# A two-layer graph network on one core: the softmax chain of a batch moved four visits later in two of three edge passes

## The reference, cut to what matters

```
m = segment_max(logits, dst); e = exp(logits - m[dst]); s = segment_sum(e, dst)
out = segment_sum(h[src] * (e / s[dst]), dst)
...
alpha = sum(xs_j * a_s) + sum(xd_i * a_d); alpha = where(alpha >= 0, alpha, 0.2 * alpha)   # layer 1
out = segment_sum(xs_j * (a * edge_weight), dst)
```

## Time and profile before

| | us |
|---|---|
| median of 3 runs | 4023.07 (4012.54 to 4028.57) |
| the profiled execution | 4020.69 |
| its span | 4018.8 |
| busy: PE / DVE / POOL / ACT | 2935.1 / 3088.3 / 2729.9 / 1446.3 |
| pass 1: first gather issued, last addition | 145.7 to 1206.2 |
| pass 3: first gather issued, last addition | 2562.9 to 3625.3 |
| mean of one L284: pass 1, 2, 3 | 1.002, 0.948, 1.006 |
| granted TensorE clock, mean | 0.85 of full |

### The profile page before, as it was taken

How to read it: one execution, slowest core, us unless ns; L and a number is a source line. 1 busy time by engine, 2 the same in 40 slices (tenths; PEclk the granted TensorE clock), 3 DMA queues, 4 the chain that set the end, 5 groups by cost and what they waited for, 6 DMA issues and landing times. The chain is left out here.

```text
span 4018.8 us, 70607 instructions
## 1 busy us (share of the span) xinstructions
PE 2935.1 (73%) x14389; PEld 2089.2 (52%) x14389; DVE 3088.3 (77%) x9652; ACT 1446.3 (36%) x4590; POOL 2729.9 (68%) x2963
## 2 busy tenths in 40 slices
PE   5456666677777677788888888466676677777998
PEld 4334444444455455555555556334444444447998
DVE  6567777788897666677777769678888899997886
ACT  2322233233326456666666666211111111112332
POOL 3577777777750277777777735577777777755886
PEclk8677777778878889999999989677778878888999
DMA  4555555555534444444444437555555555533221
GB/s 131 164 158 163 162 159 161 173 165 169 173 106 120 138 135 136 136 140 137 141 141 141 142 87 221 166 143 147 145 144 147 149 149 149 151 102 92 72 72 50
DMA packets 271620, 560.27 MB, mean 139 GB/s; under 512 B 62118, under 2 KB 164558, under 8 KB 271278
## 3 DMA queue, kind: packets, MB, share of 16 engines
q0 software_dynamic: 115872, 326.30, 29.0%
q10 hardware_dynamic: 82742, 167.20, 13.3%
q1 hardware_dynamic: 72664, 63.00, 5.4%
HBM read 478.39 MB, written 77.89 MB: 138 GB/s over the span
## 5 line engine op out<-in xcount | busy, mean ns | idle before, releaser
L475 PE MATMUL psum<-big,onehots_or_distances 128*128 128x264 f32 (+2 forms) x5280 | 1851.1, 476 | 101.9 <-DVE big L656 55.4
L475 PEld LDWEIGHTS psum<-big,onehots_or_distances 128*128 128x128 f32 x5280 | 1008.2, 223 | 281.2 <-DVE big L656 82.4
L284 POOL DMA_INDIRECT big<-table_attn,src_by_edge x782 | 741.5, 948 | 437.2 <-issue 238.0
L284 POOL DMA_INDIRECT big<-table_typed,src_by_edge x782 | 786.8, 1006 | 249.8 <-issue 237.9
L284 POOL DMA_INDIRECT big<-table_gat,src_by_edge x782 | 783.3, 1002 | 252.6 <-issue 231.8
L341 ACT ACTIVATE dot_products<-big 128x8 f32 (+1 forms) x880 | 156.5, 213 | 1562.1 <-SPq L274 1483.1
L679 DVE TENSOR_TENSOR acc<-acc,psum 128x264 f32 (+2 forms) x1320 | 558.5, 423 | 105.9 <-issue 58.6
L656 DVE TENSOR_TENSOR big<-big,psum 128x512 f32<-128x512 f32 x880 | 594.1, 675 | 14.1 <-issue 4.9
L438 PE MATMUL psum<-big,onehot_t 128*128 x2640 | 462.8, 285 | 155.1 <-SPq L274 91.7
L521 DVE SCALAR_TENSOR_TENSOR dot_products<-psum,big 128x258 f32<-128x258 f32 x880 | 367.6, 421 | 191.0 <-PE psum L438 186.4
L438 PEld LDWEIGHTS psum<-big,onehot_t 128*128 128x128 bf16 x2640 | 260.9, 101 | 362.0 <-issue 247.0
(11 more groups left out here) (284 smaller groups left out, 4243.8 us busy)
## 6 DMA issues: line engine op xcount, KB each, us to landing
onehot_t<-onehots ACTq DMA_DIRECT2D x73, 512.0 KB, 3.8
big<-visit_positions ACTq DMA_DIRECT2D x55, 512.0 KB
onehots<-big ACTq DMA_DIRECT2D x37, 512.0 KB, 5.9
big<-onehots ACTq DMA_DIRECT2D x37, 512.0 KB, 3.6
big<-in_x_dram SPq DMA_DIRECT2D x98, 128.0 KB, 2.7
big<-table_gat,src_by_edge POOLq DMA_INDIRECT x782
big<-table_attn,src_by_edge POOLq DMA_INDIRECT x782
big<-table_typed,src_by_edge POOLq DMA_INDIRECT x782
```

What stands on the lines that cost most here:

```text
L284: pool.indirect_dma_start(X[:, t % RING, :], None, ph.table, bass.IndirectOffsetOnAxis(ap=m.src[:, t:t + 1], axis=0)).then_inc(S[f"rows{t ...
L475: last = nc.tensor.matmul(sum_ps(w), onehot_at(v), rows, start=(v % 2 == 0), stop=(v % 2 == 1))
```

## The change

CHAIN_AHEAD becomes 0 for passes 1 and 3 (pass 2 does not use it). The chain's places then are the visits: it begins four visits later, `shift` goes from place 15 to 11 and so stays at visit 11, the parts from `scan_ahead` to `join_last` move from places 5..10 to 3..8 (from visits 1..6 to 3..8), and `turn_max` from place 11 to 9 (from visit 7 to 9). The expansions, the turn of the logits and the tail copies move four visits later with the batch. No instruction is added or removed, and no wait.

```diff
-        self.max_at = 13 if self.dot else 11
+        self.max_at = 13 if self.dot else 9
...
-CHAIN_AHEAD = 4
+CHAIN_AHEAD = 0
...
-                (5, 1, scan_ahead), (5, 1, scan_back), (6, 1, ends), (6, 1, turn_ends), (7, 1, run_scans), (7, 1, from_others),
-                (8, 1, join), (8, 1, carry), (9, 1, turn_joined), (9, 1, join_first), (10, 1, join_last),
-                (15, 1, shift)])
+                (3, 1, scan_ahead), (3, 1, scan_back), (4, 1, ends), (4, 1, turn_ends), (5, 1, run_scans), (5, 1, from_others),
+                (6, 1, join), (6, 1, carry), (7, 1, turn_joined), (7, 1, join_first), (8, 1, join_last),
+                (11, 1, shift)])
```

## The result

The changed kernel takes **3995.16 us** (median of 4 runs, 3986.40 to 3998.30) against 4024.80 for the kernel before in the same comparison (4 runs): ratio **0.9928 [0.9901, 0.9955]**, 29.6 us less. The forecast was 3963, 60 us less. The sign was right, the size half of what was forecast.

The account below looks back on a forecast made before the run. POOL's gather issue, lengthened by L644, was taken to bound passes 1 and 3. Terms -31 - 22 - 4.6 - 5 = -63 us, taken as -60 from 4023.1, gave 3963 us; range 3940 to 3998.

Parts of the forecast that it names:

- What bounds the kernel: Passes 1 and 3: POOL's issue of gathers sets them, 18.6 us a batch; VectorE has 2 to 3 us to spare.
- Delay = 0.55 less the distance, by L644: A gather starting within 0.55 us behind an L644 is lengthened by 0.55 us less its distance.
- The first rival: Passes 1 and 3: delays travel with the chain or come of something other than L644; -10 us, 4013; chance 0.13.
- otherwise none: Gathers that don't start within 0.55 us behind an L644 aren't lengthened: delay 0.
- Pass 1, -31 us: Pass 1: the moved L644 leave 0.2 us of gather delay a batch, 11 us for 41.7.
- Pass 3, -22 us: Pass 3: the first L644 still catches a gather, 0.42 us a batch, 23 us of delay for 45.3.
- Room in the ring, -4.6: Pass 1: POOL's twenty waits for ring room lose their 4.6 us at most, as VectorE has used up four visits more.
- The ends, -5: Ends of passes 1 and 3: plain work of four visits is already done, 2.5 us each, -5 us.
- What gets tighter, 0: Growth to shift, leaky to scan, and ScalarE's weighing have less time; cost 0, up to 2 us a batch covered.
- A check from the other side: Passes 1 and 3: L644 meeting gathers at random gives 26 us of delay a pass; random placing would give -45 us.
- the worst case of the known rule: Passes 1 and 3: a batch can lose 0.5 + 0.15 us, 35 us a pass; 17 us still gained, 3996.

Follow-up runs that it names:

- e1: Changed kernel, with pass 1's L644 reading iota from PSUM instead of SBUF: 3961.31 us, ratio 0.9847.
- e2: Kernel before the change, with pass 1's L644 reading iota from PSUM: 4000.57 us, ratio 0.9942.
- e8: Changed kernel, with L644 reading iota from PSUM in passes 1 and 3, and three sums in flight instead of four in pass 3: 3951.00 us, 0.9830.
- e5: Changed kernel, with ScalarE's two 512 KB transfers of a batch in pass 1 issued eight visits later: 4018.75 us, ratio 0.9998.
- e6: e5 with ScalarE's two long conversions of pass 1 also eight visits later: 4019.09 us, ratio 1.0004.
- e14: e9 with LAG = 8 instead of 9 in all passes: 3963.90 us, ratio 0.9857.
- e13: e8 with LAG = 8 instead of 9: 3919.66 us, ratio 0.9746.
- e17: Kernel before the change, with e13's edits (iota in PSUM in both passes, LAG = 8): 3943.64 us, ratio 0.9798.
- e11: Changed kernel, with ScalarE's weighing at v % 16 = 9 instead of 13 in passes 1 and 3: 3994.84 us, ratio 0.9919.
- e12: Changed kernel, with pass 1's chain two visits later than in the kernel before instead of four (CHAIN_AHEAD = 2): 4050.63 us, ratio 1.0052.
- e9: Changed kernel, with each of pass 1's four L644 waiting for VectorE's own instruction ahead to be complete: 3985.83 us, ratio 0.9894.
- e15: e12 with each L644 of pass 1 waiting for VectorE's own instruction ahead to be complete: 3960.15 us, ratio 0.9848.
- e4: Changed kernel, with growth (L621) as one scalar_tensor_tensor instead of tensor_scalar: 4013.30 us, ratio 0.9975.

## Why the prediction was right or wrong, point by point

- **What bounds the kernel: right.** Passes 1 and 3 go by POOL's issue of gathers; what shortened gathers shortened them.
- **Delay = 0.55 less the distance, by L644: right, but taken too narrowly.** e1, e2 and e8 show it: with one SBUF operand the delays are gone. The first rival, which the Trainium skill's inference ("SBUF — State Buffer", section "Who interferes with whom") spoke for, is contradicted by them: by it the operand could have changed nothing, and it decides over 51 us of busy time in pass 1 (792.9 to 742.2). But the rule was taken from a placing in which, in pass 1, no gather started up to 0.55 us ahead of a third or fourth L644, and **"otherwise none" is the step that failed**: it was written for all distances, negative ones included, though the earlier trace rows hold none of these. The forecast's own layout of pass 1 had such a gather. The start that it put 1.80 behind the first L644, at 3.64, is followed every 1.25 us by others, the seventh at 12.39, 0.34 ahead of the fourth L644 at 12.73, and it put "none" there. Just there 23 gathers were lengthened, nearly all by 0.88 or 0.89 us, 20.3 us in all, which is 0.55 + 0.34.
- **Pass 1, -31 us: wrong, +10.5.** The delays from behind halved (42.4 to 21.2 us, forecast 11), and 28.5 us of the new kind ate that up. And even with no delay at all pass 1 would have stood at 1005 at this placing (e1) and at 1001 at the old one (e2), not at the 984 that 41.7 us less would give, because ring room was the next bound. That bound moves with the placing as well: two visits later, with the waits, only 4.0 us of ring waits were left, and the window was 994.5. Why it moves stays open; moving ScalarE's transfers (e5, e6) raised the ring waits from 9.7 to 51.8 and 40.5 us.
- **Pass 3, -22 us: right, a little small.** -30.0. Its first L644 meets a gather as forecast, less often (43 gathers, 13.6 us, for 23).
- **Room in the ring, -4.6: wrong.** It was read as VectorE's late use; 9.7 us remain. In e14 and e13 one group less of LAG took the ring waits from 38.6 and 34.4 to 0.9 us, so there they were waits for a landing. For the kernel before itself no run tests it. The same misreading let me think that pass 1 had nothing behind its gathers but 2 to 3 us of VectorE.
- **The ends, -5: right in kind, undersized.** -8.8. The four visits were counted as plain work of 2.5 us a pass; 4.9 and 3.9 came, and in e17 against e13 5.3 and 10.6.
- **What gets tighter, 0: right.** The scan and the shift wait once each. The weighing now does make L656 wait, 174 us, which the forecast didn't see coming: it looked at the copies that the weighing is ahead of, not at the one at visit 9 that it is behind, with an arrival of the next batch. e11 shows that it costs nothing: the wait moves to the source, and the time stays.
- **"A check from the other side"** gave 4023 - 45 = 3978 for random placing, and the range's upper end was the worst case of the known rule. The result, 3995, is inside by luck: pass 1 came out 10.5 us longer where 31 less were forecast, and pass 3 and the ends, 12 us better than forecast, made up a part. At the placing of e12, 4051, the same kind of delay lies outside.

## What to carry to other kernels

If a VectorE instruction like this one, a long tensor_tensor with two SBUF operands, runs beside GpSimd's indirect gathers, first try to take an operand from PSUM. In pass 1 that took 31 us off the window at the new placing and 25 at the old one, where the change of placing alone cost 10.5. The wait for the instruction ahead helps against the delays from inside alone: 11 us (e9), but 99 at the worst placing (e15). And before a bound is called the bound, ask what the next one is: when the gathers were short, a release tied to a landing nine groups further on kept 22 and 26 us of pass 1's window, which one constant gave back (e14 against e9, e13 against e8).

## What the runs showed of the hardware

- A VectorE tensor_tensor of 0.68 us with two SBUF operands lengthened indirect gathers of 0.95 us in two ways: those that start 0.05 to 0.51 us behind it, at every place (of those 0 to 0.04 behind 14 of 92); and, at two of its four places in pass 1, those that start up to 0.5 us ahead of it (up to 2.01 us in the run two visits later). Both kinds end 1.48 to 1.53 us behind the tensor_tensor's start. The exceptions are those that start ahead of the third L644 in the changed kernel, e5 and e6, which mostly end 0.86 or 0.87 behind it. At the other places, and in pass 3, gathers ahead of it aren't touched; why is open. With a wait for the instruction ahead the second kind was not seen, with one operand in PSUM neither kind.
- It goes the other way too. L621, a TENSOR_SCALAR of 64x4, takes 0.27 to 0.28 us, but when it starts 0.4 to 0.6 us into a gather of the ordinary 0.95 it lasts until about that gather's end (0.34 to 0.53 us in the changed kernel), also where no L644 is near; as SCALAR_TENSOR_TENSOR (e4) it took 0.20 to 0.21 there. POOL and DVE of e1:

```profile
323.94 0.95 POOL L284 DMA_INDIRECT big<-table_gat,src_by_edge  x1 [0.30 <-issue]
...
324.36 0.52 DVE L621 TENSOR_SCALAR growth<-first_row,grown,cont 64x4 f32<-64x4 f32 x1
```
